# Attention and experts on one core: score operands of 72 and 74 rows, layer-norm statistics in five groups, a second sequence normalised on GpSimd

## The reference

```python
def _L0_attn_ref(x, Wq, bq, Wk, bk, Wv, bv, Wo, bo, head_mask):
    HIDDEN, HEADS = 128, 16
    HEAD_DIM = HIDDEN // HEADS
    b, s, _ = x.shape
    q = (x @ Wq.T + bq).reshape(b, s, HEADS, HEAD_DIM)
    k = (x @ Wk.T + bk).reshape(b, s, HEADS, HEAD_DIM)
    v = (x @ Wv.T + bv).reshape(b, s, HEADS, HEAD_DIM)
    attn = jnp.einsum('bqhd,bkhd->bhqk', q, k) / np.sqrt(HEAD_DIM)
    attn = jax.nn.softmax(attn, axis=-1) * head_mask[None, :, None, None]
    out = jnp.einsum('bhqk,bkhd->bqhd', attn, v).reshape(b, s, HIDDEN)
    return out @ Wo.T + bo

def _moe_forward(xf, ...):                      # 8 experts of width 512, the best 2 of each row
    shared = new_gelu(xf @ Wfc_s + bfc_s) @ Wproj_s + bproj_s
    topk_p, topk_i = jax.lax.top_k(softmax(xf @ Wr), 2)
    gate = scatter(topk_i, topk_p / sum(topk_p))
    routed = sum(new_gelu(xf @ Wfc[e] + bfc[e]) @ Wproj[e] + bproj[e]) * gate[:, e]
    return shared + routed

x = x + attention(layernorm(x))                 # x: 8 sequences x 512 rows x 128, float32
x = x + experts(layernorm(x))
```

## Time and profile before

| | |
|---|---|
| median of 3 runs | 602.75 us (602.12 to 604.01) |
| span of the profiled execution | 600.2 us |
| whole time of the profiled execution | not given apart from its span |
| PE busy | 585.2 us (98%) |
| DVE busy | 497.1 us (83%) |
| ACT busy | 452.8 us (75%) |
| POOL busy | 280.1 us (47%) |
| share of PE in the chain that ended last | 91% |

### The profile page before, as it was taken

The page is one execution under the profiler, slowest core; times in us unless marked ns, Lnnn a source line. Parts: engine busy times, 40 slices in busy tenths (PEclk is TensorE's granted clock), DMA queues, the critical chain, the costliest instruction groups (busy, mean ns, idle before and its releaser), DMA issues.

```text
span 600.2 us, 21750 instructions
## 1 busy us (share of the span) xinstructions
PE 585.2 (98%) x8258; PEld 405.9 (68%) x8258; DVE 497.1 (83%) x1076; ACT 452.8 (75%) x967; POOL 280.1 (47%) x481
## 2 busy tenths in 40 slices
PE   6898999999999999999999999999999999999997
PEld 3443556555665655655655765656899999999966
DVE  8989999999999999999999999735577777777557
ACT  5887898888888888888888888985266555555551
POOL 7947430222542542542642642656745555555500
PEclk9999999999999999999999999999999999999999
DMA  6896333324434322322322311001422222222173
GB/s 177 224 303 208 110 80 93 102 79 121 126 91 128 90 57 61 85 57 64 82 57 66 82 56 47 21 20 49 93 56 67 70 70 70 71 70 70 42 294 136
DMA packets 43839, 57.66 MB, mean 96 GB/s; under 512 B 11130, under 2 KB 31482, under 8 KB 43754
## 3 DMA queue, kind: packets, MB, share of 16 engines
q1 hardware_dynamic: 39434, 47.59, 28.1%
q0 software_dynamic: 4320, 8.89, 4.6%
HBM read 35.76 MB, written 20.42 MB: 94 GB/s over the span
## 4 chain that ended last, share of the span: by engine, by line
PE 91%; ACT 3%; SPq 2%; DMA 1%; DVE 1%; issue 1%; POOL 0%; DVEq 0%; ACTq 0%
PE ps L1423 18%; PE ps L1451 18%; PE ps L1466 18%; PE ps L1677 11%; PE ps L1665 11%; PE ps L1624 4%; PE ps L1615 4%; PE ps L1405 2%; PE ps L1655 1%; PE ps L1486 1%; ACT xn L761 1%; PE ps L1411 1%; ACT probs L774 1%; PE ps L1497 1%; ACT probs L865 1%
## 5 line engine op out<-in xcount | busy, mean ns | idle before, releaser
L1002 DVE TENSOR_REDUCE mx<-ps 128x2 f32<-128x1024 f32 x256 | 306.2, 1212 | 20.2 <-PE ps L1423 12.2
L865 ACT ACTIVATE probs<-ps 128x512 f32<-128x512 f32 x512 | 296.8, 603 | 31.5 <-PE ps L1451 13.0
L1451 PE MATMUL ps<-q_op,k_op 128*32 128x512 bf16 x2048 | 205.0, 380 | 3.0 <-DMA q_op<-mxT 2.9
L1423 PE MATMUL ps<-k_op,q_op 96*32 96x512 bf16 x2048 | 161.0, 380 | 1.8 <-DVE mx L1002 1.3
L1466 PE MATMUL ps<-probs,v_op 128*32 128x256 f32 x2048 | 160.0, 378 | 0.0
L923 ACT ACTIVATE probs<-ps,b_cur 128x128 f32<-128x128 f32 x284 | 80.8, 368 | 59.4 <-PE ps L1665 58.6
L739 POOL DMA_INDIRECT results<-rest,row_id x71 | 71.6, 1009 | 66.5 <-DVE rest L1303 48.0
L1423 PEld LDWEIGHTS ps<-k_op,q_op 96*32 96x32 bf16 x2048 | 62.1, 97 | 52.9 <-DVE mx L1002 14.2
L1466 PEld LDWEIGHTS ps<-probs,v_op 128*32 128x32 f32 x2048 | 70.9, 109 | 38.7 <-ACT probs L865 0.2
L1451 PEld LDWEIGHTS ps<-q_op,k_op 128*32 128x32 bf16 x2048 | 64.5, 95 | 46.4 <-ACT probs L865 3.1
L630 POOL DMA_INDIRECT slots<-route_sb,slot_u x64 | 63.7, 995 | 58.0 <-ACT probs L865 49.7
(11 more groups left out here) (177 smaller groups left out, 543.0 us busy)
## 6 DMA issues: line engine op xcount, KB each, us to landing
q_op<-q_scr SPq DMA_DIRECT2D x96, 96.0 KB
k_op<-k_scr SPq DMA_DIRECT2D x96, 96.0 KB
w_sb<-in_W SPq DMA_DIRECT2D x18, 256.0 KB, 3.0
probs<-slots SPq DMA_DIRECT2D x71, 64.5 KB, 1.8
q_scr<-probs SPq DMA_DIRECT2D x8, 384.0 KB, 3.8
k_scr<-probs SPq DMA_DIRECT2D x8, 384.0 KB, 3.7
k_scr<-probs SPq DMA_DIRECT2D x8, 256.0 KB, 4.4
probs<-results SPq DMA_DIRECT2D x4, 512.0 KB, 4.8
```

The costliest lines, as they stand in the source:

```text
L865: nc.scalar.activation(probs[:, i, j, :], ps[:, BANK["key", b, hg, s], :], ACT.Exp, scale=float(D) ** -0.5).then_inc(s_exp, 1)
L1002: nc.vector.reduce_max(mx[:, slot % 2, 2 * p:2 * p + 2], ps[:, bank:bank + 2, :], AX.X).then_inc(s_max, 1)
L1423: last = nc.tensor.matmul(ps[c, BK_A + a % 4, :], q_op[hg][0:SH, j, P * i + c.start:P * i + c.stop], k_op[hg][0:SH, j, :], start=True, sto ...
L1451: last = nc.tensor.matmul(ps[c, bank, :], k_op[hg][:, j, P * i + c.start:P * i + c.stop], q_op[hg][:, j, :], start=True, stop=True)
```

## The change

SH becomes 72, so that the two rows of the maximum follow the 72 rows of the parts directly. `row_scores` then runs over 72 operand partitions and `key_scores` over 74, and nothing below or behind them has to be zero. Of the settings there remain: zero in `q_op[0]` (for the warm-up), minus one in the whole `k_op` of head groups 2 and 3 by POOL, and minus one in partitions 64 to 95 of `k_op` of groups 0 and 1 by DVE (the loads then write 0 to 71 over them). The last statistics group is cut into (4, 5) and (6, 7); the fifth is taken by DVE after the v copy of sequence 2. POOL normalises sequence 1 as well as 3.

```diff
--- before.py
+++ after.py
@@ -32,7 +32,7 @@
 KR = PARTS * PR
 K_PARTS = 2 * PARTS - 1
 SHIFTS = 2
-SH = 96
+SH = PARTS * PR
 E, F = 8, 512
 NE = E + 1
 FC = F // P
@@ -233,14 +233,14 @@
         N_W1ST, N_W = 6, 5
         TILE_PARTS = (slice(0, 2 * NT), slice(2 * NT, B * NT))
         N_WFFN = 2 * NE + 1
-        N_SCR, N_ZERO, N_WARM = 3, 3, 11
+        N_SCR, N_WARM = 3, 11
         N_ROUTE = 9
         N_LD = 6
         ROWS_FROM, ROWS_EACH, MX_AT = 3, ((0, 0, 3), (1, 1, 1), (1, 1, 1), (1, 1, 0), (0, 1, 1)), 11
         LEAD, CATCH_UP = 13, ((0, 0, 15), (0, 1, 15), (1, 1, 9))
         BK_X = 0
-        LN1_SEQS = ((0,), (1,), (2, 3), (4, 5, 6, 7))
-        POOL_SEQ = 3
+        LN1_SEQS = ((0,), (1,), (2, 3), (4, 5), (6, 7))
+        POOL_SEQS = (1, 3)
         LN1_TILES = [slice(NT * some[0], NT * (some[-1] + 1)) for some in LN1_SEQS]
         LN1_OF = [n for n, some in enumerate(LN1_SEQS) for _ in some]
         UP0, DN0 = 0, 4
@@ -368,7 +368,7 @@
 
                 wait(sp, s_sb, (b * HG + hg - HG + 1) * (J * NT))
                 if b == 0:
-                    sp.wait_ge(s_zero[hg], N_ZERO)
+                    sp.wait_ge(s_zero[hg], 2 if hg == 0 else 1)
                 if hg == 0:
                     sp.wait_ge(s_scr[b % DEEP], (b // DEEP + 1) * (16 * N_SCR))
                 for r in range(PARTS):
@@ -506,35 +506,34 @@
 
                 pool.wait_ge(s_rstd, LN1_OF[b] + 1)
                 pool.wait_ge(s_nshift, LN1_OF[b])
-                pool.wait_ge(s_xnTp, b - 1)
+                wait(pool, s_xnTp, b - 1)
                 for t in range(NT * b, NT * (b + 1)):
                     last = nc.gpsimd.tensor_scalar(xn[:, b % 2, t % NT, :], x_sb[:, t, :], rstd[:, t:t + 1], neg_shift1[:, t:t + 1],
                                                    ALU.mult, ALU.add)
                 last.then_inc(s_xnp, 1)
 
-            def zero_scores(hg):
-
-                nc.gpsimd.memset(q_op[hg][:, :, :].bitcast(f32), 0.0).then_inc(s_zero[hg], 1)
-                nc.gpsimd.memset(k_op[hg][0:SH, :, :].bitcast(f32), 0.0).then_inc(s_zero[hg], 1)
+            def set_key_ones(hg):
+
+                nc.gpsimd.memset(k_op[hg][:, :, :].bitcast(f32), TWO_MINUS_ONES).then_inc(s_zero[hg], 1)
 
             nc.gpsimd.memset(neg_half[:, :], -0.5).then_inc(s_pad, 1)
-            for hg in range(2):
-                zero_scores(hg)
+            nc.gpsimd.memset(q_op[0][:, :, :].bitcast(f32), 0.0).then_inc(s_zero[0], 1)
+            for hg in range(2, HG):
+                set_key_ones(hg)
             pool.wait_ge(s_pad, 1)
             ln1_rstd(0)
             ln1_rstd(1)
-            zero_scores(2)
+            normalise(POOL_SEQS[0])
             ln1_rstd(2)
             for b in range(B):
                 if b == B - 2:
                     max_split(0)
                 third_parts(b)
                 if b == 0:
-                    normalise(POOL_SEQ)
+                    normalise(POOL_SEQS[1])
                     ln1_rstd(3)
-                elif b == 1:
-                    zero_scores(3)
                 elif b == 2:
+                    ln1_rstd(4)
                     nc.gpsimd.memset(v_op[:, :, :, :, :], 0.0).then_inc(s_pad, 1)
                     pool.wait_ge(s_pad, 2)
                     for hg in range(HG):
@@ -654,7 +653,7 @@
 
                 if b == 0:
                     pool.wait_ge(s_xnv, 1)
-                    pool.wait_ge(s_xn, B - 2)
+                    pool.wait_ge(s_xn, B - 1 - len(POOL_SEQS))
                 sl = x_sb[:, b * NT:(b + 1) * NT, :]
                 nc.gpsimd.tensor_tensor(sl, sl, bo_sb[:, :].unsqueeze(1).to_broadcast([P, NT, C]), ALU.add).then_inc(s_xbo, 1)
 
@@ -830,7 +829,6 @@
                 nc.scalar.activation(mxT[:, hg % 2, :], ps[0:SHIFTS * J * NT, BANK["mx", b, hg], 0:P], ACT.Copy).then_inc(s_mxT, 1)
 
             copy_xnT(0)
-            normalise(1)
             first_part(0, 0)
             first_part(0, 1)
             copy_xnT(1)
@@ -844,7 +842,7 @@
                     max_out(0, 0)
                 if b + 1 < B:
                     copy_xnT(b + 1)
-                if b + 2 < B and b + 2 != POOL_SEQ:
+                if b + 2 < B and b + 2 not in POOL_SEQS:
                     normalise(b + 2)
                 if b >= ROWS_FROM:
                     store_v(b)
@@ -939,7 +937,7 @@
 
             def set_key_ones(hg):
 
-                nc.vector.memset(k_op[hg][SH:P, :, :].bitcast(f32), TWO_MINUS_ONES).then_inc(s_zero[hg], 1)
+                nc.vector.memset(k_op[hg][SH - D:P - 32, :, :].bitcast(f32), TWO_MINUS_ONES).then_inc(s_zero[hg], 1)
 
             def moments(some, steps, at, part):
 
@@ -962,7 +960,7 @@
             def ln1_stats(n):
 
                 some = LN1_TILES[n]
-                dve.wait_ge(s_x[n], 16)
+                dve.wait_ge(s_x[min(n, 3)], 16)
                 for t in range(some.start, some.stop):
                     last = nc.vector.bn_stats(stats[:, t, :], x_sb[:, t, :])
                 last.then_inc(s_st, 1)
@@ -1156,8 +1154,9 @@
                 if b == 0:
                     ln1_stats(3)
                     ln1_moments(3)
-                if b in (1, 2):
-                    set_key_ones(1 + b)
+                if b == 2:
+                    ln1_stats(4)
+                    ln1_moments(4)
                 first_max(b, 2)
             def attend(b):
                 first, last = isinstance(b, int) and b == 0, isinstance(b, int) and b == B - 1
@@ -1377,7 +1376,7 @@
         @block.tensor
         def _(pe):
             pe.wait_ge(s_mxz, 1)
-            pe.wait_ge(s_zero[0], N_ZERO)
+            pe.wait_ge(s_zero[0], 2)
             for n in range(N_WARM):
                 nc.tensor.matmul(ps[:, BK_M, :], mx_parts[:, :], q_op[0][:, 0, :], start=True, stop=True)
             pe.wait_ge(s_w1st, 16 * N_W1ST)
@@ -1385,10 +1384,10 @@
             def transpose_x(b):
                 if b == 0:
                     pe.wait_ge(s_xnv, 1)
-                elif b == POOL_SEQ:
-                    pe.wait_ge(s_xnp, 1)
+                elif b in POOL_SEQS:
+                    pe.wait_ge(s_xnp, POOL_SEQS.index(b) + 1)
                 else:
-                    pe.wait_ge(s_xn, b if b < POOL_SEQ else b - 1)
+                    pe.wait_ge(s_xn, b - sum(p < b for p in POOL_SEQS))
                 wait(pe, s_xnT, b)
                 for i in range(NT):
                     last = nc.tensor.transpose(ps[:, BK_X, P * i:P * (i + 1)], xn[:, b % 2, i, :], id_sb[:, :])
@@ -1448,7 +1447,7 @@
                     pe.wait_ge(s_sh[hg], (b + 1) * (16 * SHIFTS))
                 bank = wait_for_bank("key", b, hg, s)
                 for c in QUARTERS:
-                    last = nc.tensor.matmul(ps[c, bank, :], k_op[hg][:, j, P * i + c.start:P * i + c.stop], q_op[hg][:, j, :],
+                    last = nc.tensor.matmul(ps[c, bank, :], k_op[hg][0:SH + SHIFTS, j, P * i + c.start:P * i + c.stop], q_op[hg][0:SH + SHIFTS, j, :],
                                             start=True, stop=True)
                 last.then_inc(s_sb, 1)
```

## The result

The changed kernel takes **610.25 us**, the median of 7 runs (606.35 to 612.24), against 604.01 us (602.12 to 606.21) for 7 runs of the kernel before beside them: a ratio of **1.0101 [1.0079, 1.0122]**, 1% slower. The profiled execution took 611.5 us with a span of 609.6 us; that of before had a span of 600.2 us. On another chip later the ratio was 1.0091 [1.0061, 1.0122].

What follows compares the result with a forecast made beforehand. PE was taken as the bound from about 60 us, with operand loads holding the first row scores. Terms -0.25 + 0.1 = -0.15 us gave 600.2 - 0.15 + 2.55 = 602.6 us, range 600.9 to 604.0.

Steps and rivals of the forecast that it cites:

- Fewer rows in the scores: Term for both score products: cutting 24 and 54 operand partitions changes nothing, 0 us, as matmuls took 380 ns at both sizes.
- DVE is through before 25.25: Step at the first row maximum: DVE finishes sequence 3 early, so the maximum can begin at 25.86 us instead of 26.19.
- and the moments there: Step on DVE after sequence 2: the other half of the statistics returns, 1.6 us and the moments, less 0.9 of setting.
- The 0.25 us forecast as a gain at the third pair: Term at the third pair of row scores: 0.33 us earlier by the chain, taken as 0.25 us after the semaphore's way.
- The clock falls in the prologue: Rival, 0.07: an earlier warm-up widens the gap before the transposes, the clock halves, 2.5 us lost, 605.2 us.
- a 2.1 us gap: Step before the first transposes: idle time grows from 1.53 to about 2.1 us, and such a gap passes at full clock.
- The gate opens with the compute: Rival, 0.12: operands land earlier too, the first row scores start at 23.6 us, all moves by 1.4 us, 601.3 us.
- The loads hold the first row scores: Main case, 0.72: operand loads land unmoved, so row scores start at 25.2 to 25.6 us and 1.4 us becomes waiting.
- Narrow operands make PE faster: Rival, 0.05: each of 1024 blocks of four score matmuls gains 3.5 ns, 3.6 us in all, about 599 us.
- Settings and sequence 1 on POOL: Terms in the prologue: fewer large settings and moving sequence 1 from ACT to POOL are worth 0 to the end.
- PE busy for over 99% from 100 us on: Sign that the forecast is right: PE stays busy for over 99% of the time from 100 us on.

Runs made afterwards that it cites:

- e1: The kernel before with only the score products narrowed, to 72 and 74 partitions: ratio 1.0082 [1.0061, 1.0102].
- e7: The kernel before with row scores over 72 rows, key scores still over 128, and k_op rows 0 to 95 set to minus one: ratio 1.0030 [1.0010, 1.0049].
- e8: e1 plus seven unread filler matmuls on PE between the last v projection and the first key scores: ratio 1.0053 [1.0034, 1.0073].
- e9: The kernel before with key scores over 98 rows in place of 128, row scores still over 96: ratio 1.0012 [0.9996, 1.0029].
- e3: The changed kernel with 19 warm-up matmuls in place of 11: ratio 1.0074 [1.0051, 1.0097].
- e6: The changed kernel with four statistics groups and score products over 96 and 128 partitions again: ratio 1.0000 [0.9984, 1.0017].
- e2: The changed kernel with score operands of 96 and 128 rows again and zero rows in q_op, five groups kept: ratio 1.0061 [1.0044, 1.0079].
- after_again: The changed kernel, unaltered, run once more on the chip of later experiments: ratio 1.0091 [1.0061, 1.0122].
- e11: e2 with the fifth group's statistics and moments on DVE after sequence 1 instead of sequence 2: ratio 1.0036 [1.0015, 1.0057].

## Why the prediction was wrong, step by step

- **"Fewer rows in the scores ... 0 us, both ways": wrong, and the main error.** The argument was the 380 ns at 96 and at 128 rows, and as a statement on the duration of one matmul it holds within 1 ns: 379 and 381 ns at 72 and 74. What failed is the step from the duration to the cost. Once the clock has fallen near 50 us it stays low three to four times as long over narrow operands, and the rows that hold zeros in `q_op` count in this. The term put at 0 measures 1.0082 alone, about 5 us: in e1's profile 4.7 us near 50 us and 1 us at the full clock later. The Trainium skill ("TensorEngine Tiling", section Tiling Modes) has a rule on changes of the tiling mode, which the forecast used for the same 0; no run here shows such a change, and the loss is of another kind.
- **"DVE is through before 25.25": wrong.** The fifth group was counted as 1.6 us "and the moments there", and put in the place of 0.91 us of setting without a look at what follows it in DVE's queue. The moments cost 0.74 + 1.13 - 2 x 0.17 = 1.5 us more than their size says: two of them stood beside POOL's third part and ended with its instructions. The 0.25 us forecast as a gain at the third pair became a wait of 2.53 us for 1.08. Undoing it took 1.0061 to 1.0000 with wide operands, and 1.0091 to 1.0066 with narrow ones.
- **"The clock falls in the prologue", 7%: the right mechanism, placed once and priced once.** The first fall came as written: the first projections at about twice their 1.02 us, and a first second part of sequence 0 at 14.90 us instead of 12.61. It was priced at 2.5 us; at the first row scores 1.5 us were left of it, and the falls near 30 and 50 us weren't in the forecast. It was also tied to the early warm-up, and the fall comes with the old one too (e7, e8 and e9 show it). The forecast said a 2.1 us gap passes at the full clock, taken from the end of the kernel. In the prologue it did not: the eight profiles with a first fall had idle times of 1.34 to 2.03 us before the transposes, the six without one had 0 to 1.20 us and, in before, 1.52. What PE did before a gap must be alike before one gap bounds another.
- **"The gate opens with the compute", 12%: no.** In e3, with no early fall, the row scores started at 24.82 us after 0.90 us of idle time that a DMA ended. The loads hold the first row scores, as forecast. The idle time there was forecast at 1.7 us, and the loads, forecast as unmoved, landed 0.43 us sooner.
- **"Narrow operands make PE faster", 5%: no**, as above.
- **Settings and sequence 1 on POOL, at 0: right** within e6's interval, 0.2% either way.
- **"PE busy for over 99% from 100 us on": right**, 99.88 of 100 us by the windows; that is why no gain could come from there and why the loss made before 80 us stays. That stretch didn't shrink over the narrow operands either, it grew by about 1 us.

Still open: whether the wait for DVE causes the fall near 30 us. The four profiles in which PE waited 2.2 to 2.5 us there all fell, and of the ten with 1.1 to 1.4 us one did (e8). In e2's profile, set beside before's, the first fall makes 1.0 us, the longer wait 1.2 and the second fall 1.6 up to the first key scores. Open too is which row count between 74 and 98 in the key scores is enough, and why. A kernel with five groups at a place that costs nothing wasn't found.

## What to carry to other kernels

Before rows are cut from a matmul "for free", look at the stretches where PE is coming out of idle time: look at what the granted clock does there as well as at the duration of the product, and read the mean clock of every run, not only the profiled one. When work is moved to an idle-looking slot of an engine, look at the next three instructions behind it in that queue and at who waits for them, and at what the neighbour engine runs in that slot. An idle time of PE in a prologue is priced twice: its length, and what the low clock takes if it falls there. Here 3.4 us of it near 50 us cost under 1 us, 10.2 us cost about 3 and 13.7 us about 4.5.

## What was not expected of the hardware

- Key scores over 74 of 128 operand partitions, of the same columns, count and duration as over 128, had the granted clock at 1.2 GHz for 10 to 14 us behind an idle time of 1.57 or 1.58 us, in all five profiles without fillers. With 98 and 128 rows it was down for 3.4 us (e9, e6) or not at all. The partitions left out had held zeros in `q_op`. The Trainium skill ("TensorE: Matmul & The Clock Gate", Part 1) says that activity lifts the clock; these runs add that the time to its return changed with the operand partitions, at the same columns.
- While low, the clock didn't recover under a PE that was busy for all of 6.00 us twice over (e1, 50 to 62 us). In e6 it came back after 3.4 us. The busy share in the profile doesn't tell the two apart: it was full in e6 as well, 3.20 of 3.20 us from 50.8 us on.
- A DVE operation on 128x8 took 0.74 and 1.13 us while POOL combined two 128x512 tiles, against 0.17 us: 4 to 7 times as long. The same steps, beside the same POOL line, took 0.81 and 1.13 us in e3 and 0.83 and 1.13 us in e2. In these and in after_again and e11 each such step ended within 0.04 us after the end of a POOL instruction, as if it had waited for it, while `mean`, started between two of them, took 0.16 us. What the two engines share there, no run tells.
